# A grouped convolution and a conditioned mixing of 64 samples: the mixing matrix copied inside SBUF in 16 transfers

## What is computed

```
y = x + conv1d(x, weight, 9 taps, pad 4, 4 groups) + (cond @ c_weight.T)[:, :, None] + bias
att = softmax(mlp(cond))                      # 8 numbers per sample
out = y + einsum('boi,bih->boh', sum_k att[:, k] * W[k], y) + (att @ bias_k)[:, :, None]
```

## Time and profile before

| what | value |
|---|---|
| median of 3 runs | 811.55 us (810.05 to 811.6) |
| profiled execution: its own time | 808.3 us |
| profiled execution: span of its instructions | 806.5 us |
| PE busy (matmuls) | 755.8 us, 94% of the span |
| ACT busy | 644.6 us, 80% |
| POOL busy, DVE busy | 448.7 us, 56%; 411.4 us, 51% |
| mean granted TensorE clock | 0.978 of 2.4 GHz |
| bytes moved | 177.43 MB, 220 GB/s on the mean |

### The profile page before, as it was taken

How to read it: one execution, slowest core, us unless ns; L and a number is a source line. 1 busy time by engine, 2 the same in 40 slices (tenths; PEclk the granted TensorE clock), 3 DMA queues, 4 the chain that set the end, 5 groups by cost and what they waited for, 6 DMA issues and landing times.

```text
span 806.5 us, 29186 instructions
## 1 busy us (share of the span) xinstructions
PE 755.8 (94%) x12347; PEld 669.2 (83%) x12347; DVE 411.4 (51%) x410; ACT 644.6 (80%) x460; POOL 448.7 (56%) x589
## 2 busy tenths in 40 slices
PE   3979999999999999999999999999999999999996
PEld 2759888889888988888888888889888888888895
DVE  4356446445545644564465456445545644554541
ACT  5428788888888888888888888888888888888865
POOL 1089855665565556556555655665565556556510
PEclk8779999999999999999999999999999999999998
DMA  6134677777777877877786677777777776877745
GB/s 230 45 116 141 208 237 251 209 232 260 218 221 248 258 208 228 263 232 215 236 268 211 221 256 249 213 230 262 221 222 242 254 206 229 261 214 221 253 134 176
DMA packets 66824, 177.43 MB, mean 220 GB/s; under 512 B 7850, under 2 KB 50418, under 8 KB 50418
## 3 DMA queue, kind: packets, MB, share of 16 engines
q1 hardware_dynamic: 66802, 177.10, 69.1%
HBM read 101.57 MB, written 75.50 MB: 220 GB/s over the span
## 4 chain that ended last, share of the span: by engine, by line
DMA 33%; PE 28%; ACT 21%; issue 9%; SPq 6%; DVE 1%; POOL 1%; ACTq 1%
DMA mix_dram<-mix_parts 21%; PE ps L373 14%; ACT x_ph L414 14%; PE ps L355 13%; DMA mix_rep<-mix_dram 11%; ACT z_out L435 7%; SPq L247 4%; SPq L224 1%; DMA x_in<-in_x_dram 1%; POOL mix_prod L593 1%; DVE x_lo L481 0%; POOL mix_prod L588 0%; PE ps L331 0%; ACTq L50 0%; ACTq L67 0%
## 5 line engine op out<-in xcount | busy, mean ns | idle before, releaser
L355 PE MATMUL ps<-x_hi,cw_hi 32*128 32x512 f32 x3072 | 668.7, 395 | 10.3 <-DVE x_lo L481 7.7
L355 PE MATMUL ps<-x_lo,cw_hi 32*128 32x512 f32 x3072 | 668.7, 395 | 0.0
L355 PE MATMUL ps<-x_hi,cw_lo 32*128 32x512 f32 x3072 | 667.8, 395 | 0.0
L355 PEld LDWEIGHTS ps<-x_hi,cw_hi 32*128 32x128 f32 x3072 | 476.8, 185 | 26.7 <-issue 10.9
L355 PEld LDWEIGHTS ps<-x_lo,cw_hi 32*128 32x128 f32 x3072 | 478.2, 185 | 17.4 <-issue 1.2
L355 PEld LDWEIGHTS ps<-x_hi,cw_lo 32*128 32x128 f32 x3072 | 477.6, 185 | 13.9 <-issue 0.6
L373 PE MATMUL ps<-y_hi,mix_rep 32*128 32x512 f32 x2048 | 348.3, 391 | 28.4 <-DMA mix_rep<-mix_dram 24.3
L492 DVE TENSOR_TENSOR y_lo<-ps,y_hi 128x512 fp32r<-128x512 f32 x256 | 176.6, 691 | 354.8 <-ACT y_hi L424 353.9
L373 PEld LDWEIGHTS ps<-y_hi,mix_rep 32*128 32x128 f32 x2048 | 256.6, 184 | 58.8 <-issue 48.3
L373 PE MATMUL ps<-y_lo,mix_rep 32*128 32x512 f32 x1024 | 291.7, 387 | 0.0
L435 ACT ACTIVATE z_out<-ps,par 128x1024 f32<-128x1024 f32 x128 | 257.1, 2117 | 24.8 <-PE ps L373 24.8
(11 more groups left out here) (68 smaller groups left out, 77.5 us busy)
## 6 DMA issues: line engine op xcount, KB each, us to landing
x_in<-in_x_dram SPq DMA_DIRECT2D x64, 1024.0 KB, 6.4
out_dram<-z_out SPq DMA_DIRECT2D x64, 1024.0 KB, 8.1
mix_rep<-mix_dram SPq DMA_DIRECT2D x256, 128.0 KB, 3.0
mix_dram<-mix_parts SPq DMA_DIRECT2D x64, 128.0 KB, 6.2
mixw_nat<-in_L_cond_weight_dram SPq DMA_DIRECT2D x1, 512.0 KB
cw_nat<-in_L_cond_weight_dram SPq DMA_DIRECT2D x1, 144.0 KB, 2.1
w_sb<-in_L_cond_W_dram SPq DMA_DIRECT2D x2, 64.0 KB
ctxw_nat<-in_L_cond_c_weight_dram SPq DMA_DIRECT2D x1, 64.0 KB
```

The source lines that it names most:

```text
L355: mm = pe.matmul(y_ps[:, g, :], w[rows, m, :], x_at(xx[buf(s)], rows, m), start=i == 0, stop=i == CONV - 1)
```

## The change

`mix_dram`, its store and the semaphore `mix_stored` go. SP's `load_mix` now waits for POOL (`mix_made`) and for the mixing of sample s-2, and issues 16 transfers from `mix_parts` to `mix_rep` inside SBUF, one for each band and group, 32 partitions by 1 KB. In SP's slot the order becomes: the matrix of sample s, the store of z of sample s-2, the load of x of sample s+4. TensorE's count for `mix_loaded` follows; it waits for `y_lo_made` only before the last sample's mixing, and for `z_read` only in bands 0 and 2. POOL waits for the copies instead of the store. `take_z` reads and writes the same elements in another order: position by position with the two phases innermost, where it was phase by phase.

```diff
-            def store_mix(s):
+            def load_mix(s):
 
                 if not exists(s):
                     return
                 b = buf(s)
-                made, taken = ahead(done(s), DMA * G * uses(s))
+                made, mixed = ahead(done(s), done(s, PH, lag=-2))
                 sp.wait_ge(mix_made, made)
-
-                at_least(sp, mix_loaded[b], taken)
-                sp.dma_start(mix_dram[b][:, :, :], mix_parts[b][:, :, :].bitcast(F32)).then_inc(mix_stored[b], DMA)
-
-            def load_mix(s):
-
-                if not exists(s):
-                    return
-                b = buf(s)
-                stored, mixed = ahead(DMA * (uses(s) + 1), done(s, PH, lag=-2))
-                sp.wait_ge(mix_stored[b], stored)
 
                 at_least(sp, z_ready, mixed)
                 for r in range(PH):
-                    sp.dma_start(mix_rep[b][Q * r:Q * r + Q, :, :, :].bitcast(F32).rearrange("c g h o -> c g (h o)"),
-                                 mix_dram[b].rearrange("(g c) h o -> c g (h o)", g=G)).then_inc(mix_loaded[b], DMA)
+                    for g in range(G):
+                        sp.dma_start(mix_rep[b][Q * r:Q * r + Q, g, :, :].bitcast(F32),
+                                     mix_parts[b][Q * g:Q * g + Q, :, :].bitcast(F32)).then_inc(mix_loaded[b], DMA)
...
             def slot(s):
+                load_mix(s)
+                store(after(s, -2))
                 load(after(s, AHEAD))
-                store_mix(s)
-                store(after(s, -2))
-                load_mix(s)
...
                 if i == 0:
+                    if is_sample(s, NS - 1):
+                        pe.wait_ge(y_lo_made, done(s, G))
                     if r == 0:
-                        pe.wait_ge(y_lo_made, done(s, G))
-                        pe.wait_ge(mix_loaded[buf(s)], DMA * G * (uses(s) + 1))
-
-                    at_least(pe, z_read, done(s, 2, lag=-2) + r // 2 + 1)
+                        pe.wait_ge(mix_loaded[buf(s)], DMA * G * PH * (uses(s) + 1))
+                    if r % 2 == 0:
+
+                        at_least(pe, z_read, done(s, 2, lag=-2) + r // 2 + 1)
...
-                nc.scalar.activation(z_out[buf(s)][:, :].rearrange("c (n q) -> c q n", q=PH)[:, pair, :], z_ps[:, pair, :],
+                nc.scalar.activation(z_out[buf(s)][:, :].rearrange("c (n q) -> c n q", q=PH)[:, :, pair],
+                                     z_ps[:, pair, :].rearrange("c q n -> c n q"),
                                      ACT.Identity, bias=par[s[1]][:, NK:NK + 1]).then_inc(z_read, 1)
...
-                at_least(pool, mix_stored[buf(s)], DMA * uses(s))
+                at_least(pool, mix_loaded[buf(s)], DMA * G * PH * uses(s))
```

More of the change, by code:

```diff
@@ L100, in cond_resid_kernel @@
         mix_rep = two(sb, "mix_rep", [P, G, 2, P], F32R)
-        mix_dram = [nc.dram_tensor(f"mix_dram{k}", [P, 2, P], F32, kind="Internal").ap() for k in range(2)]
         cw_hi = sb("cw_hi", [P, M, P], F32R)
@@ L182, in cond_resid_kernel @@
         mix_made = sem("mix_made")
-        mix_stored = two(sem, "mix_stored")
         mix_loaded = two(sem, "mix_loaded")
@@ L224, in load @@
                 sp.dma_start(x_in[buf(s)][:, :], x[b, :, :]).then_inc(x_loaded[buf(s)], DMA)
-            def store_mix(s):
-                if not exists(s):
-                    return
-                b = buf(s)
-                made, taken = ahead(done(s), DMA * G * uses(s))
-                sp.wait_ge(mix_made, made)
-                at_least(sp, mix_loaded[b], taken)
-                sp.dma_start(mix_dram[b][:, :, :], mix_parts[b][:, :, :].bitcast(F32)).then_inc(mix_stored[b], DMA)
             def load_mix(s):
@@ L241, in load_mix @@
                 b = buf(s)
-                stored, mixed = ahead(DMA * (uses(s) + 1), done(s, PH, lag=-2))
-                sp.wait_ge(mix_stored[b], stored)
+                made, mixed = ahead(done(s), done(s, PH, lag=-2))
+                sp.wait_ge(mix_made, made)
                 at_least(sp, z_ready, mixed)
                 for r in range(PH):
-                    sp.dma_start(mix_rep[b][Q * r:Q * r + Q, :, :, :].bitcast(F32).rearrange("c g h o -> c g (h o)"),
-                                 mix_dram[b].rearrange("(g c) h o -> c g (h o)", g=G)).then_inc(mix_loaded[b], DMA)
+                    for g in range(G):
+                        sp.dma_start(mix_rep[b][Q * r:Q * r + Q, g, :, :].bitcast(F32),
+                                     mix_parts[b][Q * g:Q * g + Q, :, :].bitcast(F32)).then_inc(mix_loaded[b], DMA)
             def store(s):
```

## The result

| | before | changed |
|---|---|---|
| median | 811.58 us (4 runs, 810.05 to 813.57) | 856.92 us (4 runs, 856.17 to 858.03) |
| profiled execution: own time, span | 808.3, 806.5 us | 857.4, 855.6 us |
| PE busy | 94% | 89% |
| ACT busy | 80% | 65% |
| bytes moved | 177.43 MB | 169.09 MB |

The changed kernel takes 1.056 times as long (95% interval 1.053 to 1.059). The forecast was 776 us; what came is what the first rival described, a pace set by SP, at nearly its time of 862.

The account below looks back on a forecast made before the run. TensorE, at 11.11 us a sample plus 0.67 us of stall, was taken as the bound; -38.7 (stall) + 3.9 (start) - 0.8 (z_out at the end) = -35.6 us, so 776.0 us for the median, range 769 to 783.

Parts of the forecast that it names:

- the first rival: SP becomes the pacemaker, issues being held behind the x_in load and z store: period 12.6 us, 862 us; chance 13%.
- What bounds the kernel before: Whole run: TensorE's own pace is 11.11 us a sample, pauses make it 11.78, an excess of 38.7 us in all.
- The ring through x_ph, store and loads: Middle of the run: mixing, z_out, x_ph, then SP's matrix store and loads wait on each other, two samples per turn.
- the stall: TensorE's mixing waiting for its matrix, 0.67 us a sample; all of it was to go, -38.7 us.
- the price of an issue: On SP: 0.48 us from issue to issue, taken from the DRAM loads, so sixteen copies take 7.6 us.
- SP's cover: SP's work of 8.6 us per sample against TensorE's 11.11 leaves 2.5 us; without it SP is the bound.
- Queued behind the copy: On SP: z's store and the x_in load, issued after the copies, still land in time, with covers of 4 and 8 us.
- POOL's wait: POOL waits for the copy, not the store: it has 9.8 us for 7.0 us of work, so no effect.
- z's reading: ScalarE's z_out in the new order takes 1.2 us, hidden in mid-run and shortening only the end, -0.8 us.
- Start: Before the first mixing: sixteen issues from 52.5 land near 62.2 where mixing had begun at 58.27, +3.9 us.
- End: After the last mixing: the last pair of z_out, 3.88 us before, becomes 1.85 + 1.2, -0.8 us.
- TensorE's dropped waits: On TensorE: no longer waiting for y_lo_made and half of z_read was taken as 0, at the most -7 us.

## Why the prediction was wrong

- **What bounds the kernel before** was right. The ring through x_ph, store and loads cost what was read off: the order alone gave 43 us, of which 38.7 had been counted as the stall. TensorE's 11.11 us is the floor in all the fast kernels.
- **The step that failed is the price of an issue**: "From issue to issue are 0.48 us", from which the text has "sixteen take 7.6 us". The row was a load from DRAM, the new operation a copy inside SBUF. It measured 0.633. That is 2.5 us more per sample and with the two held issues 3.2; SP's cover, in the paragraph that follows, was 2.5. Another 0.4 are the other two transfers, 1.4 us where 1.0 was put. The text took one price where the trace had no row for the operation, and gave it no upper end. With 2.1 us for the other two transfers and for holding, TensorE's 11.11 us leave room for 0.56 an issue, and the old period of 11.78 for 0.60; so a price a sixth higher ate the cover, and one a quarter higher the gain.
- **Queued behind the copy**: the store of z and the load of x_in were not late for anyone, as forecast. POOL's wait didn't matter either, as forecast, though the page's chain runs through it: it always made the matrix after the next.
- **Rival 1** named the engine, the direction and nearly the time, 862 for 857, but by the wrong half of its mechanism. Of the 3.6 us between 8.6 and 12.2, 2.5 are the dearer issue of all sixteen and 0.7 the two that are held; it had counted eight held at 0.5 each. It had 48 us in the middle of the run and 3 at the start; measured were 31, 4, and 14 at the end. That the sums came so near each other is luck. Its 13% came from an argument about being held alone.
- **The Trainium skill**, page DMA: Bandwidth & Descriptors, wants small transfers merged (Rules for kernel authors), and the runs agree: seven copies 766 us, sixteen 857. The same page of the Trainium skill says under Issuing engines are not separate DMA queues that the sequencer's time to initiate a DMA is usually small relative to the DMA; here an issue takes 0.59 us of the 1.86 from its start to the copy's landing, and sixteen of them 10.1 of 12.2 us a sample, and the measurement decides.
- **z's reading**: forecast 1.2 us, measured 1.195. VectorE's row was the right guide. The Trainium skill, page Advanced Engine Details and Errata, section PSUM Cachelines, says of matmuls that a pattern that isn't contiguous slows them. As a rule for ScalarE reading two banks in turn, which the prediction weighed, that does not hold: 1195 ns. In the kernel before, z_out was on the ring and the reading worth 27 us alone. With the ring gone little is left of it: seven copies with the old reading are 4 us slower, and with sixteen copies it was not tried.
- **Start**: forecast +3.9, measured +4.0, which is luck in part: fifteen pitches took 2.4 us more than forecast, but the set-up ended at 51.02 where it had been 52.51, and the last copy landed some 0.8 us sooner after its issue. **End**: forecast -0.8, measured +14.4. The text had counted TensorE's pace there, as in the earlier trace rows; but SP's order sends the copies right behind a 1 MB store, where the earlier trace rows had shown four loads taking 2.94 us, and with sixteen of them a sample's copies take over 11.4 us there too.
- **TensorE's dropped waits**: 0 forecast; with seven copies 766.09 us without them and 765.76 with them.

## What to carry to other kernels

Count a DMA queue's issues as work of an engine: number of transfers per period, times the measured pitch of that kind (source and destination), against the period that you hope to reach, not the one that you have. It costs next to nothing up to that point and its full price beyond it, so a margin that hangs on one price needs an upper bound for that price. And before a route is replaced, try the order alone: issuing the next sample's transfers before the wait that belongs to a later one gave nearly the whole gain here (768 us, against 766 for the best kernel) with no copy changed; if copies must be many, look for a layout in which they are a rotation.

## What the runs showed of the hardware

- Back to back on SP, issuing a transfer from SBUF to SBUF costs 0.59 us (0.633 start to start), for 32 to 128 partitions and 512 bytes or 1 KB each; from DRAM to SBUF 0.42 us (0.465). A store from SBUF to DRAM is issued in 0.33 to 0.36 us. The last copy of a sample lands 1.86 us after its issue starts. Copies right behind a 1 MB transfer are held, the first two together for 0.7 us; with 13 copies, which start 1.6 us later than they could, none is held (13 in 8.18 us).
- A ScalarE write of one float in four takes 2.1 us for 1024 elements; of two in four, reading two PSUM banks in turn, 1.2, which is the rate of y_hi, in order on both sides.
- VectorE's and POOL's pieces differ in length from kernel to kernel with the same shapes; whether the two lengthen each other's was not tried. In the changed kernel, VectorE's x_lo took 2693 ns and x_hi 1617 on the mean, and POOL's last sum 2194; with seven copies they are 2336, 1249 and 504. In the kernel before, POOL's write of mix_parts was long, 1139, and is 459 now:

```profile
L471 DVE TENSOR_TENSOR x_lo<-x_ph,x_hi 128x2048 fp32r<-128x2048 f32 x64 | 172.3, 2693 | 2.2
L586 POOL TENSOR_TENSOR mix_sum_f<-mix_prod 128x128 f32<-128x128 f32 x64 | 140.4, 2194 | 5.0
L593 POOL TENSOR_TENSOR mix_parts<-mix_sum_f,ident 128x128 fp32r<-128x128 f32 x64 | 29.4, 459 | 168.9 <-DMA mix_rep<-mix_parts 168.9
```

In the changed kernel nothing waited for the longer ones in the middle of the run: SP's copies set the pace, and POOL's matrices were ready a period ahead.
